# Summing two terms of an attention product in PSUM: folded values stationary, terms moved, GpSimd's sum removed

## What is computed

```python
q = split_heads(x @ Wq + bq); k = ...; v = ...
scores = einsum('bhqd,bhkd->bhqk', q, k) / sqrt(D_K)
scores = ttt_filter(scores)              # scales some scores by 1/PHI
attn = softmax(scores)
attn = attn * (sin(C1 * attn) * exp(-(attn * attn) / PHI) + cos(C2 * attn))
ctx = einsum('bhqk,bhkd->bhqd', attn, v)
h = h + ctx @ Wo + bo
```

## Time and profile before

| what | us |
|---|---|
| median of 2 runs (6780.7 and 6791.86) | 6786.28 |
| the profiled execution | 6774.6 |
| its span, first to last instruction | 6772.9 |
| TensorE busy in it | 5442.1 (80%) |
| VectorE busy | 5082.3 (75%) |
| ScalarE busy | 4262.2 (63%) |
| GpSimd busy | 2754.5 (41%) |

### The profile page before, as it was taken

How to read it: one execution, slowest core, us unless ns; L and a number is a source line. 1 busy time by engine, 2 the same in 40 slices (tenths; PEclk the granted TensorE clock), 3 DMA queues, 4 the chain that set the end, 5 groups by cost and what they waited for, 6 DMA issues and landing times. The chain is left out here.

```text
span 6772.9 us, 115321 instructions
## 1 busy us (share of the span) xinstructions
PE 5442.1 (80%) x32426; PEld 3955.2 (58%) x32489; DVE 5082.3 (75%) x10177; ACT 4262.2 (63%) x7370; POOL 2754.5 (41%) x2639
## 2 busy tenths in 40 slices
PE   2788877787777877877888777778787799997999
PEld 1455555555555555555655555555555577775777
DVE  1888888888888888888888888888888555555443
ACT  1677777777777777777777777777777322222222
POOL 4445554444555544444555444445554200100111
PEclk9888898989889888888888889888988799898999
DMA  1000000000000000000000000000000000000000
GB/s 17 12 8 7 7 7 7 7 7 10 7 7 7 7 7 7 7 9 9 7 7 7 7 7 7 9 9 7 7 7 4 8 1 2 1 1 13 4 6 6
DMA packets 34500, 48.46 MB, mean 7 GB/s; under 512 B 24473, under 2 KB 24537, under 8 KB 34010
## 3 DMA queue, kind: packets, MB, share of 16 engines
q1 hardware_dynamic: 31962, 43.49, 2.5%
q0 software_dynamic: 2048, 0.14, 0.1%
HBM read 39.40 MB, written 4.19 MB: 6 GB/s over the span
## 5 line engine op out<-in xcount | busy, mean ns | idle before, releaser
L571 PE MATMUL banks<-ident,att 128*128 128x128 f32 x8192 | 1458.9, 311 | 873.6 <-DVE ag L508 496.8
L571 PEld LDWEIGHTS banks<-ident,att 128*128 128x128 f32 x8192 | 1024.2, 159 | 1568.6 <-DVE ag L508 1044.0
L377 POOL TENSOR_TENSOR sinb<-sinb,work 128x512 f32<-128x512 f32 x1024 | 1289.3, 1272 | 900.3 <-DVE sinb L482 898.3
L599 PE MATMUL banks<-kT,qT 128*128 128x512 f32 x2048 | 1262.5, 702 | 113.9 <-ACT att L423 104.0
L387 POOL TENSOR_SCALAR wgt<-wgt 128x512 f32<-128x512 f32 x1024 | 700.2, 684 | 1586.7 <-DVE wgt L502 1581.4
L635 PEld LDWEIGHTS outp<-vo,sinb 128*128 128x128 f32 x8192 | 1164.7, 216 | 214.9 <-issue 185.3
L635 PE MATMUL outp<-vo,sinb 128*128 128x64 f32 x8192 | 1162.6, 295 | 1.9 <-ACT att L423 1.9
L476 DVE TENSOR_TENSOR work<-banks,work 128x512 f32<-128x512 f32 x1024 | 699.8, 689 | 254.0 <-ACT work L435 183.6
L451 ACT ACTIVATE work<-banks 128x512 f32<-128x512 f32 x1024 | 609.9, 596 | 420.4 <-PE banks L571 411.6
L458 ACT ACTIVATE mag<-banks 128x512 f32<-128x512 f32 x1024 | 606.4, 594 | 356.2 <-PE banks L599 350.0
L435 ACT ACTIVATE work<-banks,halfpi 128x512 f32<-128x512 f32 x1024 | 695.4, 685 | 208.9 <-PE banks L571 139.6
(11 more groups left out here) (194 smaller groups left out, 6740.6 us busy)
## 6 DMA issues: line engine op xcount, KB each, us to landing
xq<-xT_dram SPq DMA_DIRECT2D x64, 256.0 KB
xv<-xT_dram SPq DMA_DIRECT2D x64, 256.0 KB, 3.7
xT_dram<-xT SPq DMA_DIRECT2D x8, 256.0 KB, 2.9
out<-hres SPq DMA_DIRECT2D x8, 256.0 KB, 2.6
base<-in_L_tok_turns,idx POOLq DMA_INDIRECT x64
wqk<-in_L_attn_Wq SPq DMA_DIRECT2D x64, 16.0 KB
wqk<-in_L_attn_Wk SPq DMA_DIRECT2D x64, 16.0 KB
wqk<-in_L_attn_bq SPq DMA_DIRECT2D x64, 0.2 KB
```

What stands on the lines that cost most here:

```text
L377: nc.gpsimd.tensor_tensor(sinb[:, k % RING], sinb[:, k % RING], work[:, k % RING], ALU.add).then_inc(summed, 1)
L571: mm = nc.tensor.matmul(bank[:, i * P:(i + 1) * P], att[:, p, 4 * half + i, kt * P:(kt + 1) * P], ident[:], is_transpose=True, start=(i == ...
L599: nc.tensor.matmul(score_bank(n), qT[:, p, (n // 2) * P:(n // 2 + 1) * P], kT[:, p, (n % 2) * 512:(n % 2 + 1) * 512], start=True, stop=Tru ...
```

## The change

- `vo` is now the stationary operand (128x64) and the 512 columns of `work` and of `sinb` are moved through it one after the other, both summed into `outp[0:64]`: two fp32 matmuls of 512 columns per tile instead of four of 64 columns. The output is therefore transposed (64 outputs x 512 queries).
- GpSimd's addition and the semaphore `summed` go; what waited for `summed` waits for `av`, and the product waits for `acd` and `tmul`.
- Tile k is now key block k%8 and query half k//8, in the gauss stage, the sine stage and the product, so all of half 0 comes first.
- `AV[k]` is SINE+6+k for the first 8 tiles, then SINE+16+2(k-8). After each half VectorE takes `outp[0:64]` out into `acc` (copy for an even head, add for an odd one). After an odd head TensorE transposes `acc` back by 8 matmuls with the identity (`FOLD`), and VectorE adds the result to `hres` (`ADD`), once for two heads.
- `qT` and `kT` are one plane: even heads in partitions 0 to 63, odd heads in 64 to 127; the score matmul contracts over 64 partitions. `PROJ` moves from step 18 to 19.

```diff
-        qT = sb("qT", [P, 2, S])
-        kT = sb("kT", [P, 2, S])
+        qT = sb("qT", [P, S])
+        kT = sb("kT", [P, S])
+        acc = sb("acc", [D, 2, 512])
...
-        PROJ, VAL = 18, 25 + STEPS
+        PROJ, VAL = 19, 25 + STEPS
...
-        AV = [SINE + 6 + 8 * k // 5 for k in range(NTILE)]
-        OUT = AV[-1] + 1
+        AV = [SINE + 6 + k if k < TB else SINE + 16 + 2 * (k - TB) for k in range(NTILE)]
+        OUT = (AV[TB - 1] + 1, AV[-1] + 1)
+        FOLD, ADD = OUT[1] + 1, OUT[1] + 2
...
-                        k = a - SINE - 5
-                        if 0 <= k < NTILE:
-
-                            wait(pool, tmul, NTILE * g + k + 1)
-                            nc.gpsimd.tensor_tensor(sinb[:, k % RING], sinb[:, k % RING], work[:, k % RING],
-                                                    ALU.add).then_inc(summed, 1)
...
-                                wait(act, summed, NTILE * g + k - RING + 1)
+                                wait(act, av, NTILE * g + k - RING + 1)
...
-                        if a == OUT:
-                            wait(dve, av, NTILE * (g + 1))
+                        if a in OUT:
+                            half = OUT.index(a)
+                            wait(dve, av, NTILE * g + TB * (half + 1))
+                            if p == 0:
+                                nc.vector.tensor_copy(acc[:, half], outp[0:D]).then_inc(evac, 1)
+                            else:
+                                nc.vector.tensor_tensor(acc[:, half], outp[0:D], acc[:, half], ALU.add).then_inc(evac, 1)
+                        if a == ADD and p == 1:
+                            wait(dve, folded, folds(g, p) + 1)
...
-                            wait(pe, turned, TB * (g + 1))
-                            kt, half = k // 2, k % 2
+                            wait(pe, turned, TB * g + 4 * (k // TB) + 4)
+                            kt, half = k % TB, k // TB
...
-                            fill(g, p, sine_bank(k), k // 2, k % 2)
+                            fill(g, p, sine_bank(k), k % TB, k // TB)
                         if a in AV:
                             k = AV.index(a)
-
-                            wait(pe, summed, NTILE * g + k + 1)
+                            kt, half = k % TB, k // TB
+
+                            wait(pe, acd, NTILE * g + k + 1)
+                            wait(pe, tmul, NTILE * g + k + 1)
                             if k == 0:
                                 wait(pe, v_sb, g + 1)
-                            kt, half = k // 2, k % 2
-                            for i in range(4):
-                                o = (4 * half + i) * D
-                                mm = nc.tensor.matmul(outp[:, o:o + D], sinb[:, k % RING, i * P:(i + 1) * P],
-                                                      vo[:, kt, :], start=(k == 0 and i == 0),
-                                                      stop=(k >= NTILE - 2), skip_group_check=True)
-                            mm.then_inc(av, 1)
+                            if k == TB:
+                                wait(pe, evac, 2 * g + 1)
+                            nc.tensor.matmul(outp[0:D], vo[:, kt, :], work[:, k % RING],
+                                             start=(kt == 0), stop=False, skip_group_check=True)
+                            nc.tensor.matmul(outp[0:D], vo[:, kt, :], sinb[:, k % RING],
+                                             start=False, stop=(kt == TB - 1), skip_group_check=True).then_inc(av, 1)
+                        if a == FOLD and p == 1:
+                            wait(pe, evac, 2 * g + 2)
+                            for j in range(TB):
+                                mm = nc.tensor.matmul(outp[:, j * D:(j + 1) * D],
+                                                      acc[:, j // 4, j % 4 * P:(j % 4 + 1) * P], ident[0:D, 0:D],
+                                                      start=True, stop=True)
+                            mm.then_inc(folded, 1)
```

More of the change, by code:

```diff
@@ L277, in lattice @@
         names = ("consts loadq loadv projd qk_sb vald v_sb qk mags rounded kept factor filtered bias expd "
-                 "recip weights weights2 turned xpose squared gauss agd cosd acd nned sined tmul summed av outd").split()
+                 "recip weights weights2 turned xpose squared gauss agd cosd acd nned sined tmul av evac folded outd").split()
         (consts, loadq, loadv, projd, qk_sb, vald, v_sb, qk, mags, rounded, kept, factor, filtered, bias,
-         expd, recip, weights, weights2, turned, xpose, squared, gauss, agd, cosd, acd, nned, sined, tmul, summed,
-         av, outd) = (sem("l_" + n) for n in names)
+         expd, recip, weights, weights2, turned, xpose, squared, gauss, agd, cosd, acd, nned, sined, tmul,
+         av, evac, folded, outd) = (sem("l_" + n) for n in names)
         NTILE = 2 * TB
@@ L401, in projections @@
                 cols = slice(c * 512, (c + 1) * 512)
-                nc.scalar.activation(qT[0:D, p, cols], outp[0:D], ACT.Copy, scale=QSCALE).then_inc(qk_sb, 1)
-                nc.scalar.activation(kT[0:D, p, cols], outp[D:P], ACT.Copy).then_inc(qk_sb, 1)
+                rows = slice(p * D, (p + 1) * D)
+                nc.scalar.activation(qT[rows, cols], outp[0:D], ACT.Copy, scale=QSCALE).then_inc(qk_sb, 1)
+                nc.scalar.activation(kT[rows, cols], outp[D:P], ACT.Copy).then_inc(qk_sb, 1)
             projections(0, 0, 0)
@@ L447, in iteration @@
                             if d < RING:
-                                wait(act, summed, NTILE * g - RING + d + 1)
+                                wait(act, av, NTILE * g - RING + d + 1)
                             else:
@@ L549, in _, with project @@
         def _(pe):
-            pe.wait_ge(consts, 7)
-            def project(g, c):
+            pe.wait_ge(consts, 5)
+            def project(g, p, c):
                 wait(pe, loadq, 80 * (g + 1))
                 if c == 0:
-                    wait(pe, outd, g - 2)
+                    wait(pe, evac, 2 * (g - 2))
+                    wait(pe, outd, folds(g - 2, p))
                 else:
@@ L560, in project @@
                 nc.tensor.matmul(outp[:], wqk[:], xq[:, c * 512:(c + 1) * 512], start=True, stop=True).then_inc(projd, 1)
-            project(0, 0)
-            project(0, 1)
+            project(0, 0, 0)
+            project(0, 0, 1)
             def fill(g, p, bank, kt, half):
@@ L598, in iteration @@
                                 wait(pe, tmul, NTILE * (g - 2) + 13)
-                            nc.tensor.matmul(score_bank(n), qT[:, p, (n // 2) * P:(n // 2 + 1) * P],
-                                             kT[:, p, (n % 2) * 512:(n % 2 + 1) * 512],
+                            rows = slice(p * D, (p + 1) * D)
+                            nc.tensor.matmul(score_bank(n), qT[rows, (n // 2) * P:(n // 2 + 1) * P],
+                                             kT[rows, (n % 2) * 512:(n % 2 + 1) * 512],
                                              start=True, stop=True).then_inc(qk, 1)
@@ L613, in iteration @@
                                 wait(pe, agd, NTILE * g + d - 2)
[L614 removed]
+                            fill(g, p, gauss_bank(d), d % TB, d // TB)
                         k = a - SINE
@@ L643, in iteration @@
                             wait(pe, qk_sb, 4 * NHEADS if last else 4 * (g + 3))
-                            wait(pe, outd, g)
+                            wait(pe, evac, 2 * g)
+                            wait(pe, outd, folds(g, p))
                             for j in range(TB):
@@ L650, in iteration @@
                         if s == PROJ + 2 * c and (not isinstance(t, int) or t + 1 < NHEADS):
-                            project(t + 1, c)
+                            project(t + 1, 1 - par, c)
             over_heads(pe, iteration)
```

9 lines of the change are left out of this document (5 added, 4 removed).

## The result

The changed kernel takes 8136.9 us, median of 2 runs (8136.63 to 8137.16), against 6786.28 before: ratio 1.1998, 95% interval 1.197 to 1.2027. It is slower, as forecast, but by 1351 us and not by the 484 of the prediction, and it lies outside the range of 7080 to 7450.

What follows compares the result with a forecast made beforehand. Bound by VectorE in scores and gauss, a TensorE-ScalarE-VectorE ring in the sine stage, then ScalarE. Terms 6.6 + 1.0 - 0.5 + 0.3 + 0.3 = 7.7 us a head, x 64 = 493, gave 7270 us; range 7080 to 7450.

Steps and rivals of the forecast that it cites:

- the wait for L514: Scores and gauss stretch: TensorE's 2.8 us a head wait for weights row 7 goes; gain 0, bound -2.8.
- GpSimd's sum: GpSimd's 1024 additions of 1272 ns go; they ran beside other work, so value 0, bounds -0.5 and 0.
- The clock beside the exponentials: Second half of products: with no TensorE gap, full clock expected instead of 0.55; -0.5 us a head, +2.5 if half down.
- q and k in one plane: Scores: the matmul keeps the same 512 columns, so the packing costs 0.
- the clock falls: Rival: half-width stationary operand and 64-row scores bring the sine stage to clock 0.5; above 8300 us, chance 0.03.
- sine term: Sine stage: TensorE-bound 2.5 us steps, seven taking 17.5 against 10.93, +6.6 us a head; stage's end +1.0.
- Evacuation and fold: ADD +0.3 and FOLD, mostly hidden in TensorE's waits and slack, +0.3 us a head; bounds together 0.3 and 1.2.
- The gain of 0.5 beside the exponentials: Exponentials: earlier scores at full clock give -0.5 us a head; bounds -1.5 and +2.5.
- hidden: Rival: TensorE's extra 14.6 us a head slips into its idle time; 6607 us, chance 0.03.
- short records: Rival: product records take 0.246 us each in a row, product 0.98 us; +2.0 a head, 6914 us, chance 0.03.
- late scores: Rival: clock stays half beside the exponentials and scores come late, +2.5 instead of -0.5; 7470 us, chance 0.10.
- half price for 64 stationary columns: Rival: half the stationary columns halve the product to 0.86 us; +0.7 a head, 6830 us, chance 0.04.

Runs made afterwards that it cites:

- before_order: The kernel before with only the change's order of tiles (key block k%8, query half k//8), products in four matmuls as before; 6791.97 us, ratio 1.0014.
- one_term: after_padded with GpSimd's sum back and only the sum moved, one fp32 matmul of 512 columns a tile instead of two; 7004.44 us, ratio 1.0334.
- after_padded: The changed kernel with q and k in two zero-padded planes, scores contracting over 128 partitions, acc packed as 128x512, FOLD split by one semaphore; 7479.1 us, ratio 1.1011.
- before_64rows: The kernel before with one edit: q and k in one plane, scores contracting over 64 partitions; 7888.45 us, ratio 1.1632.
- short_fold: after_padded with 2 of FOLD's 8 matmuls; 7385.69 us, ratio 1.0886.
- late_evac: after_padded with the first evacuation two steps later and the second half's products one step later; 7480.24 us, ratio 1.1036.
- before_warm: The kernel before with two extra bf16 matmuls of 512 columns at the end of steps 24 to 27; 6837.79 us, ratio 1.0078.

## Why the prediction was right and wrong

Right: what bounds each stretch before; that the sine stage would be bound by TensorE; that the wait for L514 was worth nothing (before_order). That GpSimd's sum was worth nothing fits one_term, where it runs beside a full TensorE, but no run takes out the sum alone. The clock beside the exponentials was forecast at 1.00 and is 1.00, but the reason given does not hold. The prediction laid the half clock on the 1.51 us of idling ahead of score 0; one_term idles 1.54 us there and is granted 1.00. With the products of 512 columns, one or two a tile, the clock stays up there, gap or no gap; that part was luck.

Wrong, in order of size:

1. *"q and k in one plane. The score matmul has the same 512 columns; 0."* This step failed. As a duration it is right: at clock 1.00 a score takes 1.05 us from start to start with 64 rows as with 128 (changed kernel at 3031.81, after_padded at 3007.86). It asked how long the instruction takes at a given clock and not what it does to the clock. It is worth 10.3 us a head inside the change (658 us) and 17 alone (before_64rows). What could have raised the question: the stretch ran near full clock (0.91) with 128 rows of which 64 were zeros, and no row showed that stretch without them. The rival "the clock falls" named scores of 64 rows, but put the fall in the sine stage, whose seven steps had 1.00, priced it above 8300 and gave it 0.03. That the measured 8137 lies near that price is chance: the time is lost in another stretch, for another reason. The place to look was the stretch where TensorE had only scores, fills and projections.

2. *The size of the sine term.* Predicted +6.6 and +1.0, measured +8.8 to +8.9 by the marks. Seven steps took 18.48 us, not 17.5: +7.55, a step of 2.64 and not 2.5 us, inside the bounds of 2.43 to 2.73. One of them in the changed kernel:

```profile
3010.51 1.07 PE L645 MATMUL outp<-work,vo 128*64 128x512 f32 x2
3011.42 1.02 PE L647 MATMUL outp<-sinb,vo 128*64 128x512 f32 x2
3012.38 0.40 PE L594 MATMUL banks<-negI,nturn 128*128 128x128 bf16 x4
3012.61 0.61 PE L579 MATMUL banks<-ident,att 128*128 128x128 f32 x4
3013.15 1.07 PE L645 MATMUL outp<-work,vo 128*64 128x512 f32 x2
```

   The product is 0.91 + 0.96 = 1.87 us, at L1004's end of the bounds and not at the 1.75 taken, and a fill ahead of it takes 0.54. The rest of the stage is then 8.8 - 7.55 = 1.3 us longer, against the 1.0 taken.

3. *Evacuation and fold, +0.6.* Three quarters of FOLD alone are 93 / 64 = 1.5 us a head (short_fold). It was priced at full clock, 1.7 us, by records with 128 stationary rows and columns. It came at half clock with 3.92 in most heads, and at full clock it is 2.19 (late_evac), and by short_fold nearly all of it was on the path, where all but 0.6 us was thought hidden. The gain of 0.5 beside the exponentials didn't come either (from the last sine to VectorE's start it is 6.55 us in all five kernels of the table). after_padded has 52.11 - 50.18 = 1.9 us a head more than before in scores and gauss, where 0.6 was foreseen; FOLD is about 3.9 / 2 = 1.95 a head if the rest of it costs as its three quarters do, so it can be nearly all of it. But one_term has a fold too and only 51.29 - 50.18 = 1.1 more; the difference was not taken apart.

The forecast without its first error would have been 7270 for a kernel that measures 7479 (after_padded), 3% short: terms 2 and 3. The range would have missed that one too, by 29 us. The bounds were not added up in full either: the upper sum takes +0.5 for the stretch beside the exponentials where its own bound is +2.5. With it the sum is 13.4 a head, about 7630, which still lies 500 us below the changed kernel.

Of the rivals, "hidden", "short records" and "late scores" are out by the windows above: the sine stage is longer by the whole step, a record keeps its 0.43 to 0.48 us in a row of four, and the clock beside the exponentials is 1.00 with VectorE starting no later than before. The half price for 64 stationary columns is out by the same rows.

The Trainium skill, in "TensorE: Matmul & The Clock Gate" (Why this matters for your kernels), ties the clock to idle gaps between bursts. The gapless stretch beside the exponentials agrees, with 1.00, but one_term has 1.00 there with a gap of 1.54 us, so this agreement proves little. And the 28 us with TensorE busy 28.00 at 0.50 have no gap at all; here the measurement decides: a row of PE that reads full does not tell which clock is granted.

## What to carry to other kernels

Before a matmul is made narrower, or zeros that pad it are taken out, look at the stretch in which it is most of TensorE's work: the padding may be what holds the clock at 2.4 GHz, and its loss is felt in everything TensorE does there. Run that edit alone first: here it was one of several parts and cost half of the whole (658 of 1351 us). Moving an addition from an engine that waits to a matmul loads TensorE, which was not free here: compare the step of the ring with the sum of TensorE's pitches from start to start, and price them with the next instruction's load in. Price transposes and folds at both clocks, from rows of the stretch in which they will stand.

## What the runs showed of the hardware

A TensorE that is busy without a gap can stay at 1.2 GHz: 39 us of 39 in before_64rows, 28 of 28 in the changed kernel. What a matmul contracts over matters even where it is zeros: in the scores beside gauss work, 64 rows of data and 64 of zeros are granted 0.93 in after_padded, where 64 rows of data are granted 0.50. The clock falls in both; with the wide scores it comes back after some 7 us, with the narrow ones not for 44 to 47. With 96 rows it comes back too, later than with 128 (0.55 from 3038 to 3057, then 1.00).

An idle stretch of 1.54 us ahead of score 0 did not bring the clock down in one_term; about the same stretch stands ahead of 0.52 in the kernel before. What of a matmul is counted (rows, columns, records) the runs don't settle; nor whether extra wide work inside the scores would raise the clock, as no bank is free there and it wasn't tried. The extra bf16 matmuls in before_warm cut the time at half clock near them from 7.8 to 3.6 us a head.

Matmuls on different halves of the partitions can overlap. In the kernel before, each of the four engines runs its lines in the same order in all 55 heads compared. In 22 of the 32 folds of the changed kernel, though, records of FOLD (partitions 0 to 63) start between the two records of an odd head's score (64 to 127):

```profile
3053.44 1.22 PE L608 MATMUL banks<-kT,qT 64*128 64x512 f32 x1
3053.85 0.90 PE L652 MATMUL outp<-ident,acc 64*128 64x64 f32 x3
3054.45 1.05 PE L608 MATMUL banks<-kT,qT 64*128 64x512 f32 x1
```

In after_padded, where the score takes all 128 partitions, none of the 32 does. What this saves was not measured.
